# The reciprocal of the softmax sums, moved ahead of the projection's first product on VectorE

## What is computed

```python
q, k, v = split(shift(x) @ Wqkv)            # 16 heads of 64
q = l2norm(q) * qs;  k = l2norm(k) * ksc    # then rotary with a scale per position
sim = einsum('bhwie,bhwje->bhwij', q, k2) * 8     # windows of 32, keys of 2 windows
sim = where(mask, -inf, sim)
attn = softmax(sim, -1)
x = x + einsum('bhwij,bhwje->bhwie', attn, v2) @ Wo
xn = layernorm(shift(x)) * g + b
x = x + (a * gelu(gate)) @ W2 + b2          # a, gate = split(xn @ W1 + b1)
```

## Time and profile before

| | us |
|---|---|
| median of 3 runs | 5420.77 |
| lowest and highest | 5418.97, 5429.93 |
| the profiled execution's own time | 5434.1 |
| its span | 5432.2 |
| of it the network's slots, from the first to the last row maximum | 1896 to 5364 |

### The profile page before, as it was taken

The page is one execution under the profiler, slowest core; times in us unless marked ns, Lnnn a source line. Parts: engine busy times, 40 slices in busy tenths (PEclk is TensorE's granted clock), DMA queues, the critical chain, the costliest instruction groups (busy, mean ns, idle before and its releaser), DMA issues. The chain is left out here.

```text
span 5432.2 us, 158924 instructions
## 1 busy us (share of the span) xinstructions
PE 4680.3 (86%) x63808; PEld 2733.3 (50%) x63808; DVE 3515.1 (65%) x5028; ACT 3165.4 (58%) x9549; POOL 2159.0 (40%) x1582
## 2 busy tenths in 40 slices
PE   7888888777787699999999999999999999999996
PEld 3333333322232266666666566665656666666663
DVE  5666667633333377776777777776777677777774
ACT  4444444323233277766677676776777667777774
POOL 2222222200000255555555555555555555555551
PEclk9999999877777699999999999999999999999998
DMA  1000000000000232233223332232223322332222
GB/s 46 0 0 0 0 0 0 24 0 0 0 0 0 87 95 85 88 96 92 88 85 93 99 92 85 88 103 87 86 84 103 93 88 84 92 104 87 84 87 78
DMA packets 172689, 339.86 MB, mean 63 GB/s; under 512 B 38992, under 2 KB 38992, under 8 KB 170448
## 3 DMA queue, kind: packets, MB, share of 16 engines
q1 hardware_dynamic: 171984, 330.04, 19.7%
HBM read 34.19 MB, written 6.29 MB: 7 GB/s over the span
## 5 line engine op out<-in xcount | busy, mean ns | idle before, releaser
L406 ACT ACTIVATE c_Pb<-c_S,c_nb 128x64 f32<-128x64 f32 x3072 | 918.1, 325 | 678.7 <-DVE c_nb L684 678.1
L362 POOL TENSOR_TENSOR c_F<-c_tAB 128x1024 f32<-128x1024 f32 x384 | 906.4, 2360 | 222.6 <-DVE c_tAB L665 169.2
L350 POOL TENSOR_TENSOR c_Pb<-c_Pb,c_rs 128x512 f32<-128x512 f32 x384 | 400.9, 1044 | 1341.1 <-DVE c_rs L692 1341.1
L665 DVE SCALAR_TENSOR_TENSOR c_tAB<-c_PA,c_WP,c_base 128x1024 f32<-128x1024 f32 x384 | 492.6, 1283 | 315.2 <-PE c_PA L479 313.6
L406 ACT ACTIVATION_READ_ACCUMULATOR c_Pb<-c_S,c_nb 128x1 f32 x3072 | 667.1, 217 | 0.0
L665 DVE SCALAR_TENSOR_TENSOR c_tAB<-c_PB,c_WP,c_base 128x1024 f32<-128x1024 f32 x384 | 487.4, 1269 | 52.0 <-PE c_PB L479 48.4
L354 POOL TENSOR_TENSOR c_sq<-c_sq 128x512 f32<-128x512 f32 x384 | 490.6, 1278 | 2.9 <-issue 2.3
L672 DVE SCALAR_TENSOR_TENSOR c_F<-c_PD,c_F 128x1024 f32<-128x1024 f32 x384 | 466.9, 1216 | 1.4
L698 DVE COPY c_PTs<-c_S 128x512 f32<-128x512 f32 x384 | 265.7, 692 | 307.5 <-PE c_S L539 306.9
L554 PE MATMUL c_S<-c_PTs,c_VO 64*64 64x32 f32 x13824 | 441.0, 222 | 6.5 <-issue 6.5
L514 PE MATMUL c_PB<-c_WV,xf 128*64 128x256 f32 x3072 | 426.9, 396 | 11.9 <-ACT c_sq L391 7.0
(11 more groups left out here) (247 smaller groups left out, 9578.4 us busy)
## 6 DMA issues: line engine op xcount, KB each, us to landing
c_QK<-c_F SPq DMA_DIRECT2D x1536, 128.0 KB, 2.1
c_VE<-c_VO SPq DMA_DIRECT2D x384, 128.0 KB, 2.3
c_VE<-c_VO SPq DMA_DIRECT2D x384, 96.0 KB
c_stage<-in_w_heads SPq DMA_DIRECT2D x24, 256.0 KB, 3.9
c_WT<-in_w_tails SPq DMA_DIRECT2D x6, 1024.0 KB, 5.1
a_W<-in_w_level SPq DMA_DIRECT2D x1, 3335.5 KB, 11.0
c_WT<-in_w_tails SPq DMA_DIRECT2D x6, 537.5 KB, 3.7
b_W<-in_w_level SPq DMA_DIRECT2D x1, 3133.0 KB, 10.2
```

Of the source, the lines that this page charges most:

```text
L350: nc.gpsimd.tensor_tensor(p, p, rs[:, n % 2, :].unsqueeze(2).broadcast_to([P, HS, KEYS]), ALU.mult).then_inc(*p_ready.up())
L362: nc.gpsimd.tensor_tensor(F[:, j % 2], tAB[:, j % 2, 0], tAB[:, j % 2, 1], ALU.add).then_inc(*rotated.up())
L406: e = nc.scalar.activation(Pb[:, n % 2, i, :], S[:, n % 2, r, c * KEYS:(c + 1) * KEYS], ACT.Exp, bias=nb[:, n % 2, r * PS + c:r * PS + c + ...
L665: nc.vector.scalar_tensor_tensor(out=tAB[:, kind, half], in0=bank[:, :].unsqueeze(1).broadcast_to([P, 2, SEQ]), scalar=WP[:, 2 * kind + ha ...
```

## The change

In VectorE's list of a slot, `inv_sum` moves from behind product A to ahead of it. It holds for all slots of all turns; the computation is the same.

```diff
                     if tv:
                         v_copy(v, tv)
+                    if now:
+                        inv_sum(n, now)
                     if tj:
                         products(j, 0, tj)
-                    if now:
-                        inv_sum(n, now)
                     if prev and n == 6:
                         hidden(0, prev)
```

## The result

| | before | after |
|---|---|---|
| median, us | 5425.35 (6 runs) | 5393.24 (6 runs) |
| lowest to highest | 5418.97 to 5439.91 | 5389.87 to 5397.67 |
| profiled execution's span | 5432.2 | 5388.8 |
| ratio to before, 95% interval | | 0.9938, 0.9923 to 0.9953 |

The change makes the kernel 32 us faster; 63 were forecast. The time lies inside the range and the sign is right, but only half of the gain arrived. Each kernel has one trace, and its executions scatter, the slower ones at a lower mean granted clock: of the kernel before, 5405.23 us at 0.935 and 5436.47 us at 0.928. Its trace is of an execution 9 us above its median, so the two traces lie 43 us apart, not 32.

A forecast was written before the change was run, and what follows sets the result against it. TensorE bounds the network's slots, so only its idle time, some 292 us, can be saved, mostly transposes waiting for GpSimd's normalise. Terms sum to 1.37 us per turn, over 46 turns 63 us: 5357.8 us, range 5336 to 5403.

The forecast's parts named there:

- slot 2: Reciprocal starts 1.20 us earlier, so normalise ends before TensorE is free and the transposes lose their idle: gain 0.71 us.
- slot 3: Product A waits for the exponentials, mostly hidden by product B's wait for TensorE; transposes come earlier: gain 0.19 us.
- slot 4: Like slot 2, with scale ahead of v_copy; normalise about 1.2 us earlier removes TensorE's idle: gain 0.60 us.
- slot 5: The transposes' 0.19 us of idle turns into a longer wait in slot 6, behind ScalarE's chain: gain 0.
- slot 6: Product A, held by the reciprocal, is 2.10 us late; hidden(0) then delays TensorE's L594: loss 0.24 us, bounds 0 and 1.15.
- slot 7: The reciprocal no longer stands ahead of hidden(2), on the path into the last matrix products: gain 0.11 us.
- Rival 1: GpSimd's add of squares, or the DMA into QK, becomes the bound in slots 3 and 4: 5366.5 us, chance 0.13.
- Slot 7, 0 and 1: Slot 7 gains 0.11 us; slots 0 and 1 gain 0, as TensorE bounds them though normalise comes 1.5 us sooner.

The follow-up runs named there:

- f3: The kernel before the change, plus two plain fp32 products filling TensorE's idle time in slot 6: 5410.65 us, ratio 0.9969.
- f2: The changed kernel plus two plain fp32 products, overwritten by the real ones, in TensorE's idle time in slot 6: 5344.29 us, ratio 0.9847.
- e4: The kernel before, with the reciprocal ahead of product A in slot 5 alone: 5431.91 us, ratio 1.0016.
- e7: The changed kernel with nine repeated products in slot 6's idle time, and hidden(0) ahead of product A there: 5354.65 us, ratio 0.9873.
- e2: The changed kernel, but with the reciprocal back behind product A in slots 5 and 6: 5345.61 us, ratio 0.9859.
- f1: The changed kernel with the reciprocal's old place in slots 5 and 6, plus two plain fp32 products in slot 6's idle time: 5316.71 us, ratio 0.9802.
- e6: The changed kernel with the reciprocal's old place in slots 5 and 6, plus nine repeated products in slot 6's idle time: 5357.28 us, ratio 0.9875.
- e3: The kernel before, with the reciprocal ahead of product A in slot 6 alone: 5445.30 us, ratio 1.0036.
- e1: The changed kernel, but with the reciprocal back behind product A in slot 6 alone: 5363.91 us, ratio 0.9887.
- e5: The changed kernel plus nine repeated products of the second projection half in TensorE's idle time in slot 6: 5370.80 us, ratio 0.9905.

## Why the prediction was right or wrong

Against the prediction's terms, per turn in us, medians (for slot 6 the shortest tail, that is, at full clock):

| term | forecast | at full clock | as it came |
|---|---|---|---|
| slot 2 | 0.71 | 0.83 | 0.87 |
| slot 3 | 0.19 | 0.17 | 0.08 |
| slot 4 | 0.60 | 0.82 | 0.75 |
| slot 5 | 0 | 0.41, given back in slot 6 | the same |
| slot 6 | -0.24 | -0.40 | -1.01 |
| slot 7 | 0.11 | 0.07 | 0.06 |
| sum | 1.37 | 1.49 | 0.75 |

The last column is made of means; 46 x 0.75 = 35 us of the 43 that lie between the two traced executions; the medians lie 32 apart. At full clock it is 46 x 1.49 = 69 us, and f3 less f2 gave 66.

**The step that failed** is the term of slot 6: it was sized at 0.24 us with bounds 0 and 1.15, and it came to 1.01. Of this, 0.40 is the chain I had worked out, and 0.61 (a mean tail 0.54 above the shortest before, 1.15 after) is half clock. 0.61 x 46 = 28 us are nearly all of the missing 31; by the runs with the filler on both sides it is 66 - 32 = 34 us. The prediction named this sign itself: it is wrong if slot 6 grows by more than 0.24, counted from its reciprocal. I had followed one turn, in which TensorE ran on at full clock, and took L594's 1.02 us for granted; "the others repeat its pattern" was wrong for slot 6. Even its idle time was not the usual one, 1.85 us in the earlier trace rows against a median of 2.82. The median of the slot was 10.75 us before, its mean 11.28: a view of the mean, or of the spread of L594's durations, would have shown it.

**Slots 2 and 4** gained more than forecast (0.83 and 0.82 for 0.71 and 0.60), since I took TensorE's idle from the ends of the matmul rows. In slot 2 before the change, the product ahead of the transposes and the weight load of the transposes read:

```profile
3509.83 1.02 PE L571 MATMUL c_PC<-c_x1s,c 128*128 128x512 f32 x2
...
3511.57 0.42 PEld L539 LDWEIGHTS c_S<-c,c_Pb 128*128 128x128 f32 x4 [1.54 <-POOL c_Pb L350]
```

From the start of L571 to the transposes it is 1.74 us there and 0.85 us in the changed kernel (3482.99 to 3483.84), though L571's row lasts 1.02 in both: the transposes start before that row's end. So 0.89 us could be gained, neither the 0.71 of the matmul rows nor the 1.54 of the weight loads, and the gain ended where TensorE had no idle left.

**Slot 3** came near its number (0.17 of 0.19) by luck: two errors nearly cancelled. By the same distance of starts, 0.37 us could be gained there (medians). Rival 1 took 0.16 of it: the add of squares holds L501 in all 46 turns, and from the job's first product (L477) to L501 it is 0.97 us instead of 0.81. Only the new wait for the exponentials was covered as forecast, by product B's old wait for TensorE. **Slot 5** was right in its zero: the gain comes back as a wait for ScalarE's chain, shown by e4. **Slot 6's order** was right in kind, hidden(0) in front of L594 (e7), and sized too small: product A follows the reciprocal by 0.16, not 0.11, when it is held behind it, and L594 takes 1.12 instead of 1.02. **Slot 7, 0 and 1** were right.

Half clock itself: the 46 middle turns of either kernel mostly show it in runs of several turns. Before, full-clock turns of 71.6 us follow each other; after, half-clock turns of 71.4 to 71.7. A full-clock turn of the changed kernel takes 70.1, and behind it the next one falls back in the trace. The Trainium skill, TensorE: Matmul & The Clock Gate, section "What's actually happening", says that the clock has two levels, set by how busy TensorE has been recently, and that the window in which this is watched is free-running: it is not reset when a kernel starts. The trace agrees with the two levels (1.00 and 0.50 above). A free-running window would fit e4, where a longer idle time brought no more half clock, but no run here moved the idle time against it. What decides which turns go on at half clock stays open; what half clock costs is shown by f2 and f3.

## What to carry to other kernels

Moving a short instruction that releases another engine ahead of a long one is worth at most the idle time that its consumer shows, slot by slot, read from the distance between starts and not from the ends of matmul rows; in a slot where its own input comes late, everything behind it is held, so leave it in its old place there (e2 is 48 us faster than the change as made). When a saving makes TensorE's work end earlier but not its next start, look at the granted clock behind the idle time, over all turns and not one. A little useless work in such a gap can be worth it, if it is few instructions (f1: 29 us less than e2; with nine instructions instead of two, e6, nothing was gained).

## What the runs showed of the hardware

- Half clock behind TensorE's idle times of 2.8 to 3.2 us came in 17 to 42 of 46 turns, in one trace of each kernel: with 2.8 us in 18 (before), 28 (e3) and 29 (e2), with 3.2 us in 17 (e4), 36 (e1) and 42 (the changed kernel). With 0.7 us left (e6) or 1.1 us (e5, e7, f1, f3) it came in none, with 1.5 us in 10 (f2).
- At half clock L594's two fp32 passes took 2.02 us instead of 1.02 to 1.12, and the mask products L526 0.64 instead of 0.38.
- Nine added products in a list of TensorE let an unrelated line stand 2.8 to 3.9 us with no releaser, in slot 4 of one turn in eight (e5, e6, e7); with two added products (f1, f2, f3) it stood in no slot 4 for over 0.5 us. The cause is not shown.
- A reciprocal of 8 values per partition takes 0.19 to 0.20 us and lets the next VectorE instruction start 0.11 to 0.16 us behind it.
- TensorE's transposes started 0.85 us behind the start of a two-pass product of 512 columns whose row lasts 1.02 us: the rows' ends are not when the engine is free.
